# A graph network of four layers on one core: the last two blocks of both gather passes written out, the last one with 7 chunks

## The reference

```python
    edge_index = jnp.stack([src, dst])
    x = _layernorm(x + _L0_gnn_ref(x, src, dst, edge_type_64, edge_weight1, ...), axis=-1)
    x = _layernorm(x + _L1_gnn_ref(x, edge_index, ...), axis=-1)
    x = _layernorm(x + _L2_gnn_ref(x, src, dst, edge_attr_32, ...), axis=-1)
    x = _layernorm(x + _L3_gnn_ref(x, edge_index), axis=-1)

# L0: per edge the row of its source and type, times its weight, summed per target
        msg = node_feats[src] * norm
        seg = etype.astype(jnp.int32) * N + dst
        s = jax.ops.segment_sum(msg, seg, num_segments=R * N)
        h = jnp.einsum('rni,rio->no', s, W) + bias
# L2: per edge a small network of source, target and edge features, summed per target
        msg_in = jnp.concatenate([nodes[row], nodes[col], edge_features], axis=-1)
        messages = _mlp(msg_in, mW1, mb1, mW2, mb2)
        aggregated = jax.ops.segment_sum(messages, col, num_segments=nodes.shape[0])
```

## Time and profile before

| | us |
|---|---|
| median of 3 runs | 11435.95 |
| the profiled execution | 11445.84 |
| its span, first to last instruction | 11442.9 |
| PE busy | 6980.6 |
| DVE busy | 6860.1 |
| POOL busy | 6424.7 |
| ACT busy | 2795.3 |
| granted TensorE clock, mean | 0.767 of full speed |

### The profile page before, as it was taken

One profiled execution on the slowest core, in us unless ns is written; L12 is line 12 of the kernel. 1 busy time (PEld: TensorE's weight loads), 2 busy tenths in 40 slices (PEclk: granted clock), 3 DMA queues, 4 the chain that ended last, 5 costly groups with the idle time before them and its releaser, 6 DMA issues. The chain is left out here.

```text
span 11442.9 us, 147532 instructions
## 1 busy us (share of the span) xinstructions
PE 6980.6 (61%) x54285; PEld 5438.7 (48%) x54333; DVE 6860.1 (60%) x8420; ACT 2795.3 (24%) x2578; POOL 6424.7 (56%) x6751
## 2 busy tenths in 40 slices
PE   9955555555555555699999999443434333333435
PEld 4433333333333333599989999332323233333324
DVE  5488888888888888422232222566666656565665
ACT  4333333333333333300000000222221212121212
POOL 4377777777777777100000000577777777777775
PEclk9966767767666766899999999766666666666667
DMA  9933333333333333599979998444444444444443
GB/s 385 392 123 129 127 129 127 132 125 134 123 134 123 134 124 132 180 355 355 356 270 356 356 356 317 122 113 107 113 108 112 110 110 111 109 112 108 113 107 75
DMA packets 588593, 2032.55 MB, mean 178 GB/s; under 512 B 195913, under 2 KB 354051, under 8 KB 463235
## 3 DMA queue, kind: packets, MB, share of 16 engines
q1 hardware_dynamic: 310210, 1292.34, 33.5%
q0 software_dynamic: 207360, 318.92, 12.2%
q10 hardware_dynamic: 70944, 420.31, 10.1%
HBM read 1396.53 MB, written 634.49 MB: 177 GB/s over the span
## 5 line engine op out<-in xcount | busy, mean ns | idle before, releaser
L1252 POOL DMA_INDIRECT big<-Pd,mt x3240 | 3062.2, 945 | 1077.3 <-issue 987.2
L402 POOL DMA_INDIRECT big<-Yd,ix x3240 | 3062.2, 945 | 1017.8 <-issue 987.2
L496 PE MATMUL ps<-ring 128*128 128x490 bf16 x3240 | 1420.7, 538 | 1711.5 <-DVE ring L438 1711.5
L1363 PE MATMUL ps<-big 128*128 128x384 bf16 x2160 | 567.7, 425 | 2497.2 <-DVE big L1286 2497.2
L435 DVE TENSOR_TENSOR ring<-ps,vw 128x2940 bf16<-128x2940 f32 x540 | 1736.3, 3215 | 480.2 <-PE ps L498 479.9
L496 PEld LDWEIGHTS ps<-ring 128*128 128x128 bf16 x3240 | 418.5, 129 | 2475.5 <-issue 1629.9
L1363 PEld LDWEIGHTS ps<-big 128*128 128x128 bf16 x2160 | 246.3, 120 | 2720.0 <-DVE big L1286 2528.9
L629 PE MATMUL ps<-big,cb 128*128 128x192 bf16 x13230 | 1115.2, 246 | 0.0
L629 PEld LDWEIGHTS ps<-big,cb 128*128 128x128 bf16 x13230 | 1084.7, 98 | 11.4
L516 ACT ACTIVATE Z<-ps 128x1470 bf16<-128x1470 f32 x544 | 778.3, 1467 | 1254.1 <-PE ps L498 1254.1
L516 ACT ACTIVATE big<-ps 128x1470 bf16<-128x1470 f32 x536 | 766.5, 1468 | 1267.4 <-PE ps L498 1267.4
(11 more groups left out here) (218 smaller groups left out, 11670.8 us busy)
## 6 DMA issues: line engine op xcount, KB each, us to landing
Yd<-big SPq DMA_DIRECT2D x196, 1024.0 KB, 8.8
Aj<-Z SPq DMA_DIRECT2D x68, 2940.0 KB, 9.5
big<-Aj SPq DMA_DIRECT2D x136, 1470.0 KB, 8.4
cb<-Aj ACTq DMA_DIRECT2D x136, 1470.0 KB, 8.5
Aj<-big SPq DMA_DIRECT2D x67, 2940.0 KB, 9.5
cb<-Aj SPq DMA_DIRECT2D x134, 1470.0 KB, 8.4
Z<-Aj ACTq DMA_DIRECT2D x134, 1470.0 KB, 8.4
dr<-in_dstr SPq DMA_DIRECT2D x137, 1152.0 KB, 7.7
```

Source lines behind the costliest of these rows:

```text
L402: e.indirect_dma_start(gv[j][:, k, 0:64], None, table, bass.IndirectOffsetOnAxis(ap=ix[j][:, k:k + 1], axis=0)).then_inc(sm[f"g{j}"], 16)
L496: nc.tensor.matmul(PS[q][:, 0:W * NT], olo[r][:, c, :], one[r][:, c, :], start=True, stop=False)
L1252: e.indirect_dma_start(gv[j][:, k, :], None, Pd, bass.IndirectOffsetOnAxis(ap=mt[j][:, k:k + 1], axis=0)).then_inc(sm[f"g{j}"], 16)
L1363: last = nc.tensor.matmul(ag, oh[j][:, k, :], parts[q][:, 3 * P * c:3 * P * (c + 1)], start=(k == 0), stop=(k == K - 1))
```

## The change

Both gather passes use a new helper `short_blocks`, which writes out blocks 133 and 134 behind a loop that runs 66 times. With that a turn of the code can tell which block it is when the program is built. In block 134 (KL = 7 chunks, TL = 3 triples):

- POOL issues 7 gathers.
- Typed pass: DVE builds two of the four groups, a target one-hot of 7 chunks, and multiplies 7 chunks; it prepares no next block. TensorE does 9 chunks of the products and 7 of the sum, ACT 3 triples, and SP stores `aj` behind the third triple. The store has the same size as before.
- Wide pass: all engines do the first third only; TensorE sums 7 chunks, and in block 133 it computes one third for block 134 and not three. DVE prepares nothing.
- Blocks 135 and 136 are not loaded.

On the host, padding edges get sources that are spread over the nodes (a stride of 97) in place of 0; their targets and their type are as before.

```diff
+KL = -(-E // P) - (NB - 1) * K
+        def short_blocks(e, turn):
+            turn(0, 0, 0)
+            with e.Fori(0, NB // 2 - 1, 1) as i:
+                turn(2 * i + 1, 1, i)
+                turn(2 * i + 2, 0, i + 1)
+            turn(NB - 2, 1, NB // 2 - 1)
+            turn(NB - 1, 0, NB // 2)
+
+        def at(b, n):
+            return type(b) is int and b == n
...
+            TL = -(-KL // 3)
...
                 def store(b, j, i):
-                    e.wait_ge(sm["av3"], reg(e, 2 * b + 2))
+                    if at(b, NB - 1):
+                        e.wait_ge(sm[f"av{(TL - 1) % 4}"], 2 * b + (TL + 3) // 4)
+                    else:
+                        e.wait_ge(sm["av3"], reg(e, 2 * b + 2))
...
-                    for k in range(K):
+                    for k in range(KL if at(b, NB - 1) else K):
                         e.indirect_dma_start(
                             gv[j][:, k, 0:64], None, table,
                             bass.IndirectOffsetOnAxis(ap=ix[j][:, k:k + 1], axis=0)).then_inc(sm[f"g{j}"], 16)
-                blocks(e, turn)
+                short_blocks(e, turn)
...
-                    nc.vector.tensor_tensor(oh, bc_t(iof[:, 0:P], K, P), bc_f(rl[j][:, :], K, P), ALU.is_equal)
-                    e.wait_ge(sm["cm2"], c1)
-                    group(j, 2, n)
-                    if last:
+                    nc.vector.tensor_tensor(oh[:, 0:kn, :], bc_t(iof[:, 0:P], kn, P), bc_f(rl[j][:, 0:kn], kn, P), ALU.is_equal)
+                    if not last:
+                        e.wait_ge(sm["cm2"], c1)
+                        group(j, 2, n)
+                    if not first:
                         add(b - 1, 1 - j)
-                    weight(1 - j)
-                    e.wait_ge(sm["cm0"], c2)
-                    group(j, 3, n)
-                    e.wait_ge(sm[f"g{j}"], 16 * K * i + 16 * K)
-                    nc.vector.tensor_tensor(gv[j][:, :, 0:64], gv[j][:, :, 0:64], bc_f(pw[j], K, 64),
+                    if not last:
+                        weight(1 - j)
+                        e.wait_ge(sm["cm0"], c2)
+                        group(j, 3, n)
+                    e.wait_ge(sm[f"g{j}"], 16 * K * i + 16 * kn)
+                    nc.vector.tensor_tensor(gv[j][:, 0:kn, 0:64], gv[j][:, 0:kn, 0:64], bc_f(pw[j][:, 0:kn], kn, 64),
                                             ALU.mult).then_inc(sm["mul"], 1)
...
-                    for t in range(TR):
+                    for t in range(TL if at(b, NB - 1) else TR):
...
-                    if before:
+                    if not first:
                         add_parts(b)
-                    prep(1 - j, 16 * (i + 1 + j), reg(e, b + 2), 16 * b + 32)
-                    if before:
+                    if not last:
+                        prep(1 - j, 16 * (i + 1 + j), reg(e, b + 2), 16 * b + 32)
+                    if not first:
                         add(b - 1, b)
-                    e.wait_ge(sm[f"g{j}"], 16 * K * i + 16 * K)
+                    e.wait_ge(sm[f"g{j}"], 16 * K * i + 16 * (KL if last else K))
                     gather(0, j, n)
+                    if last:
+                        middle(0, n)
+                        low(0, n)
+                        return
...
+                    nxt = 1 if at(b, NB - 2) else 0 if last else ST
...
-                    for q in range(ST):
+                    for q in range(1 if last else ST):
                         e.wait_ge(sm[f"o{q}"], n)
-                        agg(j, q)
-                        if q == 0:
+                        agg(j, q, KL if last else K)
+                        if q == 0 and nxt:
                             e.wait_ge(sm[f"f{1 - j}"], 48 * (i + j) + 48)
-                        pre(1 - j, q)
+                        if q < nxt:
+                            pre(1 - j, q)
...
-    src, dst, typ = (_blocks(g[n], f) for n, f in (("src", 0), ("dst", FAR), ("edge_type_64", 0)))
+    src, dst, typ = (_blocks(g[n], f) for n, f in (("src", np.arange(NPAD + 2 * EB) * 97 % N), ("dst", FAR),
+                                                   ("edge_type_64", 0)))
```

More of the change, by code:

```diff
@@ L384, in sync @@
                 load(1, 1)
[L385 to L390, removed]
+                short_blocks(e, turn)
                 for j in range(2):
-                    e.wait_ge(sm[f"m{j}"], 16 * (NB // 2 + 1))
+                    e.wait_ge(sm[f"m{j}"], 16 * (NB // 2 + 1 - j))
                     e.wait_ge(sm[f"o{j}"], 16 * (NB // 2 + 2 - j))
@@ L449, in turn @@
                 def turn(b, j, i):
-                    last, b = type(b) is not int, reg(e, b)
+                    first, last, b = at(b, 0), at(b, NB - 1), reg(e, b)
                     n, c0, c1, c2 = reg(e, b + 1), reg(e, 2 * b), reg(e, 2 * b + 1), reg(e, 2 * b + 2)
-                    if last:
+                    kn = KL if last else K
+                    if not first:
                         e.wait_ge(sm["cm2"], c0)
@@ L484, in turn @@
                 def turn(b, j, i):
-                    before, b = type(b) is not int, reg(e, b)
+                    first, last, b = at(b, 0), at(b, NB - 1), reg(e, b)
                     n, done = reg(e, b + 1), [reg(e, 2 * b + h) for h in range(3)]
-                    for k in range(K):
+                    for k in range(3 * TL if last else K):
                         g, c, t = k // GC, k % GC, k // 3
@@ L493, in turn @@
                         if k % 3 == 0:
-                            if t >= 2 or before:
+                            if t >= 2 or not first:
                                 e.wait_ge(sm[f"av{(t + 2) % 4}"], done[(t + 2) // 4])
@@ L497, in turn @@
                         pr, pc = (r, c - 1) if c else (1 - r, GC - 1)
-                        last = nc.tensor.matmul(PS[q][:, 0:NT], olo[pr][:, pc, :], oex[pr][:, pc, :], start=False, stop=True)
+                        mm = nc.tensor.matmul(PS[q][:, 0:NT], olo[pr][:, pc, :], oex[pr][:, pc, :], start=False, stop=True)
                         if k % 3 == 2:
-                            last.then_inc(sm[f"cm{t % 4}"], 1)
+                            mm.then_inc(sm[f"cm{t % 4}"], 1)
                     e.wait_ge(sm["mul"], n)
[L502 to L505, removed]
+                    kn = KL if last else K
+                    for k in range(kn):
+                        mm = nc.tensor.matmul(ag[j], gv[j][:, k, :], oh[:, k, :], start=(k == 0), stop=(k == kn - 1))
+                    mm.then_inc(sm["pe"], 1)
+                short_blocks(e, turn)
             def scalar(e):
@@ L1345, in turn @@
                     middle(2, n)
-                    load(b + 2, j)
+                    if type(b) is not int or b + 2 < NB:
+                        load(b + 2, j)
                 load(0, 0)
                 load(1, 1)
-                blocks(e, turn)
+                short_blocks(e, turn)
             def tensor(e):
@@ L1358, in pre, with agg @@
                     last.then_inc(sm[f"p{q}"], 1)
[L1360 removed]
+                def agg(j, q, chunks=K):
                     for c in range(C):
                         k = C * q + c
[L1363 to L1365 removed]
+                        if k < chunks:
+                            last = nc.tensor.matmul(ag, oh[j][:, k, :], parts[q][:, 3 * P * c:3 * P * (c + 1)],
+                                                    start=(k == 0), stop=(k == chunks - 1))
+                    if C * (q + 1) >= chunks:
                         last.then_inc(sm["ag"], 1)
```

51 lines of the change are left out of this document (27 added, 24 removed).

## The result

| | before | after |
|---|---|---|
| median of 5 runs, us | 11433.96 (11431.57 to 11437.68) | 11377.75 (11377.5 to 11378.41) |
| span of the profiled execution, us | 11442.9 | 11375.9 |
| mean granted TensorE clock | 0.767 | 0.770 |

The ratio is 0.995, with a 95% interval of 0.9936 to 0.9965: 56.2 us less. The forecast was 11379, its range 11370 to 11391. The direction and the size are as forecast; of the steps that set the end of the typed pass two were off, in opposite directions.

The account below looks back on a forecast made before the run. POOL's issuing, 1250 ns a gather, was taken to set the pace of the gather passes. Gains of 24.9 us (typed) and 32.3 us (wide) sum to 57.2, from 11435.95 to 11378.8 us, range 11370 to 11391.

Parts of the forecast that it names:

- What bounds the passes: Both gather passes: POOL's issuing sets the pace, 1250 ns a gather, 30.0 us a block.
- The backlog of one-row reads: Block 134, both passes: reads of one row fall behind issuing, leaving 10.3 us (typed) and 10.0 us (wide).
- The typed pass: End of the typed pass: gain of 24.9 us, range 18.9 to 32.5, with the last store as last event.
- Up to VectorE's second group nothing moves.: Typed pass, block 134: the group still starts at 4594.49 and ends at 4599.25.
- The landing of 9.5: Typed pass: the last store, issued at 4602.5, takes 9.5 us and lands at 4612.0.
- The last addition ends near 4604.4: Typed pass, block 134: VectorE's last addition ends then, beside the store, and matters only if 7.6 us late.
- The wide pass: End of the wide pass: it ends at 11301.1 against 11333.37, a gain of 32.3 us, range 30 to 34.
- Written-out blocks at 0: Blocks 133 and 134 written out behind the loop: cost taken as 0, with 5 us a pass kept for the range.
- Rival 2: Written-out blocks stall at their first run, 5 us in each pass: gain 47.2, time 11388.8; chance 0.06.
- rival 3: A loop's code no longer stays at hand and each turn fetches: slower, 11714 us; chance 0.03.
- The sum: Whole kernel: 24.9 us typed plus 32.3 us wide, a gain of 57.2 us, giving 11378.8 us.
- block 134's spread sources at 0: Block 134, chunk 7: spreading the sources of its 44 padding edges brings 0 us.

Follow-up runs that it names:

- experiment 1: Kernel before, with only the padding edges' sources spread over the nodes, all 24 chunks still gathered and computed: 11416.14 us, ratio 0.9984.
- Experiment 4: Kernel before, with the change in the wide pass alone, typed pass as before, padding reading row 0: 11402.46 us, ratio 0.9973.
- experiment 3: Kernel before, with the change in the typed pass alone, wide pass as before, padding reading row 0: 11410.09 us, ratio 0.998.
- experiment 5: The whole change, except that the padding edges' sources stay 0: 11376.22 us, ratio 0.9948 to the kernel before.
- experiment 6: The change, with the typed pass's last-store wait moved to before the next phase's first write to its buffer: 11372.18 us, ratio 0.9942 to before.
- 7: The change, with VectorE's second group of block 134 cut from 6 chunks to 3: 11374.39 us, ratio 0.9945 to the kernel before.
- experiment 8: The change with both the moved last-store wait and the second group cut to 3 chunks: 11371.83 us, ratio 0.9942 to the kernel before.
- 2: Kernel before, with block 134's gathers cut to 7 in both passes, its other work left, padding reading row 0: 11408.74 us, ratio 0.9977.

## Why the prediction was right, point by point

**What bounds the passes** was right: POOL's issuing, 1.25 us a gather. On the slow chip it is no longer so, and the change gains there too.

**The backlog of one-row reads** was right in cause and size: experiment 1 takes 11.4 and 10.7 us off the two waits (10.3 and 10.0 were derived), with the share down from 0.88 to 0.13. The last store falls from 15.4 to 8.4 when nothing but the read rows changes, so the reads held it up, as forecast. But the trace before does not show the two taking turns. The store was issued at 4618.40; these are the packets of the gathers' queue (q0) and the stores' (q1) in the two stretches 4618 to 4626 and 4626 to 4630 us (packets, MB, share of 16 engines):

```profile
q0 software_dynamic: 155, 0.15, 82.4%
q1 hardware_dynamic: 6, 0.14, 4.1%
```

```profile
q1 hardware_dynamic: 76, 1.79, 103.7%
q0 software_dynamic: 10, 0.00, 0.1%
```

A store has 144 packets. In experiment 1, without the backlog, the first of them move within 0.9 us of the issue. Here, while the backlog lasted, it got 6 of them through beside 155 of the gathers, and the rest only when the backlog was gone. Experiment 4, with the same reads, has the same: 5 beside 157, then 77 beside 11. The Trainium skill (DMA: Bandwidth & Descriptors, section SWDGE vs HWDGE vs iDMA) says that the engine takes turns between the queues of software- and hardware-generated DMAs. With turns packet by packet the store should have moved about as many packets as the gathers; it did not, so on this the trace does not bear the rule out. The late landing that I had explained by the rule was there, but it came about in another way: the store waited the backlog out. What inside the engines makes it wait, and what makes reads of one row slow, no run here shows.

**The typed pass**, 24.9 forecast, 24.4 alone in experiment 3 and 23.2 between the two traces. Three steps were mis-sized, counted from block 134's first gather:
- "Up to VectorE's second group nothing moves." It starts 9.25 us behind block 134's first gather before and 11.71 after. TensorE's sum of block 133 took 7.84 us here and 5.46 before, at a granted clock of 0.68 against 1.00:

```profile
4584.21 7.84 PE L520 MATMUL ps<-big 128*65 128x128 f32 x48 [0.93 <-DVE big L487]
```

```profile
4584.00:4592.00 8.00, 7.79 (x49) 7.77 (x50) 4.83 (x4) 0.71 (x1) 4.41 (x5) 0.68 0.86 337
```

  In experiment 5, with the same code, that sum takes 5.60 us at a clock of 1.00 (4584 to 4592) and the group starts 9.54 us behind the first gather. So executions of one code differ by 2.2 us here, and a step read from one trace carries about that much. It may not be chance alone: in the other traces whose typed pass is written out (3, 6, 7, 8) the group starts at 11.51, 11.45, 10.84 and 10.97, and in the other ones with block 134's work as before (1, 2, 4) at 10.18, 9.38 and 9.37. With one trace each this stays open. The store went out at 19.9 instead of 17.3, 2.6 later.
- The landing of 9.5: this store landed in 8.4, the low end of its row. That gives 1.1 back. With 1.1 instead of 0.9 from the landing to SP's next DMA the misses are 2.6 - 1.1 + 0.2 = 1.7, which is 24.9 less 23.2.
- "The last addition ends near 4604.4", 19.2 behind the first gather. It ends at 4604.32, but the gathers began 4.0 earlier, so that is 23.1: 2.3 from the late group, and 1.6 more because TensorE's sum of the seven chunks and the addition took 4.9 and not 3.3. The prediction took 7 of 24 of a sum that ran in part at the full clock (0.50, then 0.96 from 4632 us on); the short sum took 3.25 us, all of it at 0.50. In experiment 8 it took 1.74 at 1.00. All this was hidden under the store, as the prediction said it would be up to 7.6; in experiment 6, where the store is not waited for, it is what decides.

**The wide pass**, 32.3 forecast, 32.0 found (32.05 in experiment 4). Every sub-step lies within 1 us: reduction at 17.0 us behind the first gather (16.0; TensorE's 16 matmuls between its first and second sum took 3.45, and 2.45 before), 1.3 to the first addition (2.0), 5.9 to the sum (5.8), 2.42 for seven matmuls (2.4), 1.5 for the end (2.0). The misses, 1.1 us too short and 1.2 too long, nearly cancel.

**Written-out blocks at 0** was right within what the runs resolve. POOL's gap at block 133 and 134 is 0.30, and no other engine shows a gap with releaser issue at block 133 in either pass. Rival 2 (11388.8), a stall of 5 us a pass, is false, and so is rival 3 (11714): the two passes over Aj, from the first matmul to the last, take 2365.0 us against 2365.6. What is left of a doubt is the later start of VectorE's group, above, 1 to 2 us in the typed pass. The Trainium skill (Runtime: NRT & Kernel Launch, section Instruction fetch mechanics) says that instructions are fetched ahead in order, by which code behind a loop comes ahead of need; the trace agrees, with two fetches more and no gap.

**The sum**, 57.2, is 56.2 by the medians. That it is off by 1 us only is in part luck: the steps missed by 1 to 2.6 us each and in opposite directions, and the interval of the ratio reaches from 40 to 73 us. I had put block 134's spread sources at 0 in the written-out kernel, and experiment 5 can't tell them from 0.

## What to carry to other kernels

A ragged end of a stream is worth its full chain, not its share of the instructions: look at the last wait before each barrier and name the next late thing before counting a gain. Padding that points an indirect read at one row is not free; spread it, and it costs what real data costs. When a store is what a barrier waits for, move that wait to the first place that needs it (here the first write to its buffer), and expect the next loads to be slower beside it; here 4 us were left, on one chip.

## What was not expected

- 128-row gathers of one and the same row keep the DMA engines busy 0.88 of the time at 20 GB/s, 0.21 at 27 GB/s over eight rows, and 0.12 to 0.14 at 23 to 26 GB/s over rows of real edges or of the whole table.
- The pace of the same gathers differs between executions: 1.24992 and 1.24838 us, 9.9 us over the kernel.
- One of the three chips of the experiments ran the same kernel in 14196 us for 11434 to 11438, with the gather passes slower and the passes over Aj not.
- A 2,940 KB store issued behind a backlog of such reads got 6 of its 144 packets through in 8 us and landed in 15.4, for 8.4 with the reads spread.
